# Row and column attention: x transposed raw while it loads, then one fused pass

## The reference

```python
g = group_norm(x, 32 groups of 6 channels, over rows and columns)
msa = transpose(g, (0, 2, 1, 3))                      # (1, C, R, E)
Qs = (msa[:, :, 0] @ Wq_s) / sqrt(D); Ks = msa @ Wk_s
sw = softmax(Qs @ Ks over R, seq_mask)                # a weight for each row, column and head
Q = (g @ Wq) * SCALING / sqrt(C) * sw; K = g @ Wk; V = g @ Wv
attn = softmax(einsum('brihd,brjhd->bhij', Q, K), res_mask)   # 192 x 192 for each head
out = x + einsum('bhij,brjhd->brihd', attn, V)
```

## Time and profile before

| | us |
|---|---|
| median of three runs (626.15 to 629.93) | 629.26 |
| the profiled execution | 631.34 |
| its span, first to last instruction | 629.5 |
| PE busy, 5368 matmuls | 505.7 |
| DVE busy | 422.6 |
| ACT busy | 252.1 |
| POOL busy | 225.3 |
| mean granted TensorE clock, share of full speed | 0.904 |
| moved by DMA, 152.84 MB | 243 GB/s |

### The profile page before, as it was taken

One profiled execution on the slowest core, in us unless ns is written; L12 is line 12 of the kernel. 1 busy time (PEld: TensorE's weight loads), 2 busy tenths in 40 slices (PEclk: granted clock), 3 DMA queues, 4 the chain that ended last, 5 costly groups with the idle time before them and its releaser, 6 DMA issues.

```text
span 629.5 us, 15205 instructions
## 1 busy us (share of the span) xinstructions
PE 505.7 (80%) x5368; PEld 403.9 (64%) x5368; DVE 422.6 (67%) x1029; ACT 252.1 (40%) x555; POOL 225.3 (36%) x231
## 2 busy tenths in 40 slices
PE   0030198999649999999998999869499997999794
PEld 0020177998525555555546998758399997998683
DVE  2899848699945766767663666846266663667764
ACT  0030136678416666666652113223255652122232
POOL 1010024478503433434341000547166663001484
PEclk9996557799659999999998999979699998999988
DMA  8993004699965998989999999999878757999998
GB/s 275 407 434 163 0 1 118 190 265 273 265 199 165 247 279 247 265 259 246 264 230 194 283 293 279 284 331 263 276 228 263 255 162 158 298 288 283 298 257 227
DMA packets 206876, 152.84 MB, mean 243 GB/s; under 512 B 169648, under 2 KB 189680, under 8 KB 206064
## 3 DMA queue, kind: packets, MB, share of 16 engines
q1 hardware_dynamic: 154912, 132.14, 72.1%
q10 hardware_dynamic: 51920, 20.11, 12.6%
HBM read 95.60 MB, written 56.62 MB: 242 GB/s over the span
## 4 chain that ended last, share of the span: by engine, by line
PE 58%; DVE 18%; DMA 7%; SPq 5%; issue 4%; ACTq 3%; ACT 2%; POOL 2%; POOLq 0%; DVEq 0%
PE PS L990 19%; PE PS L1000 10%; PE PS L1051 7%; DVE EXTRA L603 7%; DVE BIG L849 5%; PE PS L882 3%; PE PS L1080 3%; PE PS L1081 3%; PE PS L1084 3%; PE PS L1082 3%; PE PS L1083 3%; PE PS L921 2%; DMA v_scratch<-EXTRA 2%; DVE EXTRA L709 2%; ACTq L575 2%
## 5 line engine op out<-in xcount | busy, mean ns | idle before, releaser
L449 POOL TENSOR_TENSOR BIG<-EXTRA,BIG 128x192 f32 (+1 forms) x144 | 106.7, 742 | 148.7 <-ACT BIG L519 147.1
L990 PE MATMUL PS<-WP,EXTRA 128*128 128x384 f16 (+1 forms) x1152 | 152.0, 291 | 9.5 <-DMA EXTRA<-xt_scratch 8.7
L990 PEld LDWEIGHTS PS<-WP,EXTRA 128*128 128x128 f16 x1152 | 103.0, 99 | 55.7 <-issue 11.0
L773 DVE TENSOR_TENSOR EXTRA<-PS,SW 128x192 f32<-128x192 f32 x192 | 63.8, 353 | 93.1 <-ACT BIG L534 56.1
L1051 PE MATMUL PS<-BIG,EXTRA 128*128 128x256 f16 x768 | 90.2, 281 | 11.3 <-ACT EXTRA L581 11.2
L457 POOL TENSOR_TENSOR BIG<-BIG,EXTRA 64x512 f32<-64x512 f32 x36 | 45.1, 1265 | 137.0 <-DVE BIG L849 109.0
L1051 PEld LDWEIGHTS PS<-BIG,EXTRA 128*128 128x128 f16 x768 | 76.4, 101 | 24.2 <-issue 10.7
L1000 PE MATMUL PS<-WP,EXTRA 64*128 64x384 f16 (+1 forms) x1152 | 78.0, 285 | 1.1 <-ACT SW L514 1.0
L440 POOL TENSOR_TENSOR BIG<-EXTRA,BIG 128x1024 f16<-128x1024 f32 x24 | 52.7, 2199 | 72.4 <-ACT BIG L490 72.3
L530 ACT CAST EXTRA<-PS 128x384 f16<-128x384 f32 x96 | 46.2, 481 | 54.4 <-PE PS L1000 25.6
L1000 PEld LDWEIGHTS PS<-WP,EXTRA 64*128 64x128 f16 x1152 | 50.0, 95 | 26.7 <-issue 10.0
(11 more groups left out here) (150 smaller groups left out, 692.2 us busy)
## 6 DMA issues: line engine op xcount, KB each, us to landing
EXTRA<-xt_scratch SPq DMA_DIRECT2D x48, 512.0 KB, 3.8
BIG<-in_x SPq DMA_DIRECT2D x6, 3072.0 KB, 21.1
xt_scratch<-BIG SPq DMA_DIRECT2D x48, 256.0 KB, 4.4
EXTRA<-xt_scratch SPq DMA_DIRECT2D x48, 256.0 KB, 4.0
v_scratch<-EXTRA SPq DMA_DIRECT2D x32, 384.0 KB, 4.4
BIG<-v_scratch SPq DMA_DIRECT2D x16, 768.0 KB, 6.6
BIG<-in_x SPq DMA_DIRECT2D x12, 768.0 KB, 9.6
out_x<-BIG ACTq DMA_DIRECT2D x12, 768.0 KB, 7.5
```

The source lines that it names most:

```text
L449: pool.tensor_tensor(QA[:, :, bass.ds(SI[h] * n + low, SI[h])], TQ[h][g % 4], QA[:, :, bass.ds(SI[h] * n, SI[h])], ALU.subtract).then_inc( ...
L773: ins = v.tensor_tensor(tq[:, :, :, i:i + 2], pq.rearrange("p i (m d) -> p m d i", d=D), swv[:, :, i:i + 2].unsqueeze(2).to_broadcast([P, ...
L990: ins = mm(po, xs0, WP[:, w, 0, wc], start=opens and i < 2 and j == 0, stop=not opens and j == 2, skip_group_check=True)
```

## The change

- x is loaded in 24 chunks of 8 columns into a ring of six slots (XR). PE transposes each chunk raw, ACT copies all three tiles out of PSUM into BIG (`copy_raw`), and DVE takes the statistics by channel from the transposed copy: three instructions of 512 elements for a chunk. The 15 weight pieces become 18.
- The sums over groups become nine float32 matmuls with one moving column each (`add_groups`), twice. They give scale and shift by channel directly.
- One pass follows, written out for 24 chunks. For chunk c + 3 DVE normalises in place (`normalise_x`), ACT casts (`xn_high`), POOL makes all low parts (`xn_low`). For chunk c + 2 PE makes the scores (`scores`), and ACT, DVE and PE do the softmax of 96 columns of scores (`scores_low`, `score`, `scores_transposed`, `score_max`, `exponent`, `normalise_weights`, `weights_back`, `row_weights`). For chunk c PE projects four groups (`project0`) from the tile on chip, and the copies of stage 4 follow (`kv_high0`, `q_high0`, `low0`, `q_low0`). PSUM buffers of the projection: three, where there were four.
- The score vectors are made in four groups, with the queries spread by head (`queries_by_head`, `score_vectors`).
- The split chunks are still stored to HBM, in one DMA a chunk, and loaded once, for heads 6 to 11.
- Q and K lie in another order: Q by head, column, channel; K by head, 16-column block, channel, column. The stationary operand of the logits is now read with a step of 16 elements, 32 bytes. Its fifth matmul goes to columns of its own in PSUM, and ACT copies it too.

```diff
-            for c in range(NXC):
+            for c in range(NCH):
                 if c == 1:
                     sp.wait_ge(s_wld, 16 * N_WEIGHTS)
-                sp.dma_start(X[:, c * XC * E:(c + 1) * XC * E],
-                             xs[:, c * XC:(c + 1) * XC, :].rearrange("r c e -> r (c e)")).then_inc(s_x[c], 16)
+                when(sp, s_tr, c - NSLOT + 1)
+                sp.dma_start(XR[c % NSLOT], xs[:, c * CI:(c + 1) * CI, :].rearrange("r c e -> r (c e)")
+                             ).then_inc(s_x[c % NSLOT], 16)
...
+            def copy_raw(c):
+                act.wait_ge(s_tr, c + 1)
+                nc.scalar.copy(raw(c), PS[:, 3 * (c % 2):3 * (c % 2) + 3, :].rearrange("p t (q n) -> p (t q) n", n=P)
+                               ).then_inc(s_raw, 1)
...
             for c in range(NCH):
-                if c in U_AT:
-                    k = U_AT.index(c)
-                    act.wait_ge(s_u, k + 1)
-                    u_out(nc.scalar, PS[:, 6:8, :], k, True).then_inc(s_uh, 1)
-                act.wait_ge(s_tr, c + 1)
...
+                if c + 1 < NCH:
+                    exponent(c + 1)
+                for g in range(NQ):
+                    kv_high0(c, g)
+                    if c or g:
+                        q_high0(c - (g == 0), (g - 1) % NQ)
+                    if g == 0 and c + 3 < NCH:
+                        xn_high(c + 3)
+                    if g == 1 and c + 1 < NCH:
+                        row_weights(c + 1)
+                    if g == 2 and c + 2 < NCH:
+                        scores_low(c + 2)
...
+            def normalise_x(c):
+                for t in range(3):
+                    v.tensor_scalar(raw(c, t), raw(c, t), abc[:, t:t + 1], abc[:, 3 + t:4 + t],
+                                    ALU.mult, ALU.add).then_inc(s_n, 1)
...
             for c in range(NCH):
...
+                if c + 3 < NCH:
+                    normalise_x(c + 3)
+                for g in range(NQ):
+                    low0(c, g)
+                    if g == 0 and c + 1 < NCH:
+                        normalise_weights(c + 1)
+                    if g == 2 and c + 2 < NCH:
+                        score(c + 2)
+                if c + 2 < NCH:
+                    score_max(c + 2)
...
+            def add_groups(a, s):
+                for b in range(3):
+                    for t in range(3):
+                        ins = mm(GS[:, a, b:b + 1], GM[:, t, b, :], s[:, t:t + 1], start=t == 0, stop=t == 2)
+                return ins
...
+            def scores_transposed(c):
+                pe.wait_ge(s_se, c + 1)
+                when(pe, s_sex, c)
+                when(pe, s_sw, c)
+                nc.tensor.transpose(STP, SCO, ident[:, :]).then_inc(s_stt, 1)
+
+            def weights_back(c):
+                pe.wait_ge(s_snm, c + 1)
+                when(pe, s_sw, c)
+                nc.tensor.transpose(SWP, EXPO[0:CI * H, :], ident[0:CI * H, 0:CI * H]).then_inc(s_swt, 1)
...
+            for c in range(NCH):
+                project0(c, 0)
+                if c == 0:
+                    scores_transposed(1)
+                project0(c, 1)
+                if c + 1 < NCH:
+                    weights_back(c + 1)
+                if c + 2 < NCH:
+                    scores(c + 2)
+                project0(c, 2)
+                project0(c, 3)
+                if c + 2 < NCH:
+                    scores_transposed(c + 2)
...
-                        p0, p1 = PS[:, 2 * (k % 2), 0:C], PS[:, 2 * (k % 2) + 1, 0:C]
-                        kh, kl = KA[:, m, 0:C], KA[:, m, C:2 * C]
-                        mm(p0, QA[:, m, 0:P], kh, start=first, stop=False)
...
+                        q0, q1, q2 = (QA[:, k, t * P:(t + 1) * P, d] for t in range(3))
+                        kh, kl = (KA[:, k, t * NB_HI:(t + 1) * NB_HI, d, :] for t in range(2))
+                        mm(p0, q0, kh, start=first, stop=False, skip_group_check=True)
+                        mm(p0, q0, kl, start=False, stop=last, skip_group_check=True)
+                        mm(p1, q1, kh, start=first, stop=False, skip_group_check=True)
+                        mm(p1, q1, kl, start=False, stop=last, skip_group_check=True)
+                        ins = mm(p2, q2, kh, start=False, stop=last, skip_group_check=True)
```

More of the change, by code:

```diff
@@ new lines, in row_column_attention, with v_stored, projected0, projected1 @@
+        NG0 = C // 2
+        NG1 = C // 4
+        TURNS = NCH // 4
+        def v_stored(c):
+            return sum(32 if b < P // CI else 64 for b in range(c % 2, c + 1, 2))
+        def projected0(s):
+            b = 2 * (s % 3)
+            return PS[:, b:b + 2, :]
+        def projected1(g):
+            b = 2 * ((g + 3) % 4)
+            return PS[:, b:b + 2, :].rearrange("p a (b n) -> p b a n", b=2)
+        def k_pair(c, g, low):
+            c0 = (c % 2) * CI + 2 * g
+            return KA[:, :, c // 2 + low * NB_HI, :, c0:c0 + 2]
@@ new lines, in q_high0 @@
+            def q_high0(c, g):
+                s = NQ * c + g
+                act.wait_ge(s_tq[0], s + 1)
+                nc.scalar.copy(QA[:, :, 2 * s:2 * s + 2, :], tq0(s).rearrange("p i k d -> p k i d")
+                               ).then_inc(s_qh[0], 1)
+            xn_high(0)
+            u_high(0)
+            xn_high(1)
+            u_high(1)
+            scores_low(0)
+            u_high(2)
+            xn_high(2)
+            u_high(3)
+            exponent(0)
+            scores_low(1)
@@ L596, in step, with statistics @@
                 dve.wait_ge(s_dve, count[0])
[L599 to L603 removed]
+            def statistics(c):
+                dve.wait_ge(s_raw, c + 1)
+                for t in range(3):
+                    ins = v.bn_stats(ST[:, t, c, :], raw(c, t))
@@ new lines, in _ @@
+            normalise_x(0)
+            queries_by_head()
+            normalise_x(1)
+            u_low(0)
+            normalise_x(2)
+            u_low(1)
+            score(0)
+            u_low(2)
+            score_max(0)
+            u_low(3)
+            normalise_weights(0)
+            score(1)
+            score_max(1)
+            for c in range(NCH):
+                if c + 3 < NCH:
+                    normalise_x(c + 3)
+                for g in range(NQ):
+                    low0(c, g)
[5 more added lines that the diff above has]
+                    score_max(c + 2)
@@ L963, in _ @@
[L963 to L974 removed]
+                pe.wait_ge(s_raw, NCH)
@@ new lines, in half_rows, with project0 @@
+            def half_rows(outs, xt, q, wc, first, last):
+                for j, (s, w) in enumerate(((0, 0), (0, 1), (1, 0))):
+                    for a, rows in ((0, slice(0, E1)), (1, slice(E1, P))):
+                        ins = mm(outs[a], xt[rows, 1, s, q * P:(q + 1) * P], WP[rows, 1, w, wc],
+                                 start=first and j == 0, stop=last and j == 2, skip_group_check=True)
+                return ins
+            def project0(c, g):
+                s = NQ * c + g
+                when(pe, s_kvl[0], s - 2)
+                if s < 3:
+                    pe.wait_ge(s_ul, 2 * UG)
+                ps = projected0(s)
+                xt = TT[c % 4].rearrange("p (t s n) -> p t s n", t=3, s=2)
+                outs = [ps[:, a, 0:CW[0]] for a in range(2)]
+                parts = (full_rows, half_rows) if s % 2 == 0 else (half_rows, full_rows)
+                for j, part_of in enumerate(parts):
+                    ins = part_of(outs, xt, g, slice(0, CW[0]), j == 0, j == 1)
+                ins.then_inc(s_pj[0], 1)
```

1020 lines of the change are left out of this document (490 added, 530 removed).

## The result

The changed kernel takes **634.02 us** (median of 20 runs, 629.66 to 637.5), the kernel before 629.69 in 20 runs beside it: ratio **1.0062** [1.004, 1.0083]. It is a little slower (0.6%), where 619 was forecast. Its profiled execution took 634.45 us, span 632.7.

A forecast was written before the change was run, and what follows sets the result against it. DVE was taken to bound the load, PE the projection, two waiting rounds the new pass. Start to 109 plus pass 218 puts logits at 327 against 337.5: 631.3 - 10.5 + 0.6 = 621.4 profiled, 2.1 less for the median, 619; range 604 to 632.

The forecast's parts named there:

- Load and statistics: Start, loading x: DVE's 69 statistics instructions at 0.59 us set the pace; last statistic at 68 us, 1 us sooner.
- Score vectors: Before the pass: 64 instructions, 20 us at the low clock, 10 at the high one; 15 taken.
- Group sums: After the statistics: nine float32 matmuls make 18 loads, 4.5 us, done twice; +8 us against before.
- From the statistics to the vectors, and behind them: Start: last statistic at 68, pass at 109; first scores, first softmax and waits estimated at 6 us (3 to 10).
- The pass: 24 chunks from first project0 to logits: 9.1 us a chunk instead of 6.07, 218 us in all.
- both waits where they were named: PE in each chunk: weights_back waits for normalise_weights (4.9 us, group 0 to 2), scores_transposed for score (4.2 us).
- Strided load: Logits: stationary operand with a 32-byte step costs nothing; rival that it becomes the bound, 641 us, chance 0.25.
- Its sign of being wrong: Logits: the forecast is wrong if the stationary loads last over 0.1 us.
- `normalise_x` beside POOL: Rival in the pass: DVE's normalise_x waits for a POOL instruction each time, 23 us, 642 us; chance 0.12.
- the sign of 0.5: Pass: the forecast is wrong if normalise_x takes over 0.5 us an instruction.
- The clock while x loads: Rival at the start: PE's clock stays low, transposes at 2.7 us a chunk set the load, +20, 639 us; chance 0.10.
- The rounds that don't bind (575): Rival in the pass: softmax steps are ready when PE comes, pass 174 us instead of 218, 575 us; chance 0.10.

The follow-up runs named there:

- gm_on_dve: Changed kernel with the three group-matrix copies out of PSUM moved from ACT to DVE: 625.7 us, ratio 1.0 to the kernel before.
- half_vectors: Changed kernel with the columns of all score vectors halved, half of the scores left wrong: 628.4 us, ratio 0.9985 to the kernel before.
- busy_fill: Changed kernel with unused float16 matmuls of 512 columns around the group sums and ahead of the score vectors, where PE waits: 624.7 us, ratio 0.9954.
- scores_first: Changed kernel with PE doing the scores of chunk c+2 before the waiting transpose of chunk c+1's row weights: 619.4 us, ratio 0.9877.
- late_softmax: Changed kernel with every softmax step in the pass moved half a chunk later: 614.8 us, ratio 0.9825 to the kernel before.
- late_both: late_thirds with the row weights scaled on ACT behind group 2 instead of on DVE behind group 1: 596.2 us, ratio 0.945 to the kernel before.
- late_thirds: late_softmax and gm_on_dve together, with x normalised in thirds behind groups 1 to 3, a whole chunk ahead: 615.2 us, ratio 0.9737.
- all_four: late_both with the filler matmuls of late_fill: 587.4 us, ratio 0.9338 to the kernel before.
- late_fill: late_softmax and gm_on_dve together, with busy_fill's matmuls and six more ahead of each later call of score_vectors: 595.7 us, ratio 0.9437.
- late_moved: late_softmax and gm_on_dve together, row weights scaled on ACT, normalise_x in thirds between groups, xn_high and xn_low moved: 621.7 us, ratio 0.99.

## Why the prediction was wrong

The time was 15 us over the forecast, which is the 15.1 us by which the logits began late (342.1 against 327).

- **Load and statistics: failed, 68 against 79.6.** The prediction had "Chunk 1 is transposed and copied at about 23.3; 69 instructions are 40.7 and the small DVE work between them some 4". The 0.59 us an instruction was right (0.595). Wrong was that DVE would be fed. The prediction never walked the PE and ACT queues ahead of the first transpose: three copies behind ACT's issues and a table load, for which it had no term. gm_on_dve and the runs built on it show some 8 of the 11.6 us. For the rest, PE's wait for the weights' maximum and ACT's scaling between raw copies are in the trace, but no run took them away; it stays open.
- **Score vectors: mis-sized, 15 against 26.5.** I had taken the middle between 20 cold (the low clock) and 10 warm (the high one). It was all cold, and cold was 25.8 for the 16 pairs, 0.40 us an instruction and not 0.28 x 144/128. The rate came from matmuls with stationaries of 32 rows and 96 or 192 columns, scaled by columns; half_vectors shows that halving the columns takes 0.35 off 1.61 us. The warm pair (0.91 in busy_fill) makes 14.6, so the warm end of 10 was 4.6 short, and the 15 that I took would have been right only for a clock that was never there.
- **Group sums: about right.** 4.5 us each forecast, 4.0 measured, at the low clock; the first took 2.17 behind fillers.
- **From the statistics to the vectors, and behind them.** 19 us forecast for the first, 18.7 measured. 6 for first scores, first softmax and waits; 2.6 lie behind the last vector and 0.7 between the calls, so 2.7 less than forecast. That hid a part of the two errors above.
- **The pass: right.** 9.1 forecast, 8.92 measured, with both waits where they were named. scores_first and late_softmax show that these rounds, not an engine, set it: the work is the same and only its order differs. PE's own work came out at 7.3 (the usual chunk of late_both) and not 7.1.
- **Strided load: taken as 0, was 0**, though the load is 46 ns dearer; the prediction had 57 in hand. Its sign of being wrong, loads that last over 0.1, came true (144 ns) and meant nothing: a load already lasted 98 ns before, with one matmul every 82.
- **`normalise_x` beside POOL: the rival did not happen in the change** (547 ns mean, a little over the sign of 0.5; three in 1.45 us, with no POOL instruction in their way in the chunk at 149 us), but its mechanism came with late_softmax and late_thirds, on L764 and L728.
- **The clock while x loads** was 0.74 to 0.92 between 20 and 50 us, and 1.00 from 50 on. The rival said that transposes at the low clock would set the load; from 52.78 DVE set it.
- **The rounds that don't bind (575)** were excluded by the written order, as the prediction said. With other orders the chunk comes near PE's own: late_both has 7.32.

The balance as it came out: 114 us of separate stages removed, against statistics that end 10.5 us later, 47.8 us from there to the first `project0`, and a pass of 214.7 instead of 154.5. That is 4.6 us lost.

## What to carry to other kernels

Before you sum the instructions of a new first stage, walk each engine's queue from its first entry to the first one of that stage: a setup copy behind DMA issues delayed the whole first stage by some 8 us. Where a chunk's steps form a round over several engines, the order in which each queue holds them is worth as much as the work (8.92 to 8.09 us a chunk here by order alone, to 7.32 with one small operation moved to another engine as well). Price a matmul from a row with the same stationary operand and type, at the clock level the engine will have there, not by its columns.

## What the runs showed of the hardware that I had not expected

- Float32 matmuls that kept PE busy 10.00 of 10 us ran 26 us at a granted clock of 0.50, with nothing but 0.7 us of other work between them. In busy_fill it was 0.50 until 90 us and rose there, behind eight float16 matmuls of 512 columns that began at 85.44 (3.57 us) and two float32 ones; the ten at 91.43 ran at 1.00 (2.33 us). At 104 us it fell again, within float32 work that had begun at 94. Six between the calls kept it at 1.00 in all_four; in late_fill it fell once at 88.7 and came back within the next six.
- A DVE instruction from SBUF to SBUF with one tensor operand took 0.28 us alone and 1.18 when it started within a POOL subtraction of 1.16; one of 512 elements took 0.53 and up to 1.51 (late_moved). "SBUF — State Buffer" of the Trainium skill (SBUF: two separate sides) describes a port pair that either holds for its whole instruction; these rows agree.
- A 128 x 128 float16 stationary read with a step of 32 bytes loaded in 144 ns, contiguous in 98.
